# The odd 96 rows of layer 2's gate and up weights: one shared weight, the rest of up in full fp32

## The chip, the cores and the metric

One core of a Trainium2 chip runs the whole program. The metric is device time in microseconds (us) of one execution. The kernel before takes 410.91 us, the median of 3 runs (410.29 to 411.19).

## The reference, cut to what matters

There are 1024 tokens with 512 features, all in fp32. Each of the two layers ends in a layer norm, and each contains a gated feed-forward part. Layer 1's has 1248 hidden rows, layer 2's has 1376, that is 10 full chunks of 128 rows and an odd chunk of 96. Layer 2's weights go through a 4-bit quantisation and back, in blocks of 64 elements.

```python
# layer 1
delta = x @ gate_w.T - local_point
approx_out = approx_up @ local_approx_output.T + sum over m of (delta**m / m! * approx_up) @ fuse_weight[:, :, m-1].T
ffn_out = silu(x @ ffn_gate_w.T) * (x @ ffn_up_w.T) @ ffn_down_w.T        # 1248 rows
x = layernorm(x + approx_out + ffn_out)
# layer 2
dq1, dq2, dq3 = (nf4_quant_dequant(w) for w in (w1, w2, w3))               # 1376 rows
h = silu(x @ dq1.T) * (x @ dq2.T)
x = layernorm(x + h @ dq3.T)
```

## The kernel before

**Products.** Nearly every fp32 product is made of three matmuls in the reduced fp32 format: each operand is split into a high and a low part, and hi·hi, hi·lo and lo·hi are added up in PSUM (`product`, L1291 to L1294). Only one product is done in full fp32 with a single call per piece, `project_up` (L1325 to L1332).

**The order on TensorE.** (1) The pre-stage, (2) layer 1's pairs, (3) layer 1's second stage in two passes, one for each half of the tokens, (4) layer 2's pairs, (5) layer 2's second stage in two passes. A pair is one chunk of hidden rows for one half (512) of the tokens: 4 slices of features times 3 matmuls for gate into one PSUM bank, and the same for up into the next, 24 matmuls in all. Layer 1 has 20 pairs, layer 2 has 22. In layer 2, chunk 10 (96 rows) comes last, as pairs 20 and 21. Its matmuls have 96 columns of weight in place of 128.

**Layer 1's odd chunk** (96 rows, its pairs 0 and 1) is done otherwise. `project_first` (L1316) takes all 96 rows of gate and the last 32 of up as one weight of 128 columns, 12 matmuls for each half. `project_up` then takes up's first 64 rows in full fp32: for each of 4 slices one matmul for either token half, the first half's output on partitions 0 to 63 of a bank, the second's on 64 to 127. It uses the raw weight and the raw x.

**Behind the pairs.** In layer 1, ScalarE applies silu to the gate bank (L680) and VectorE multiplies by up (L917, L920). In layer 2, ScalarE applies silu (L680) and copies up's bank into one of two SBUF buffers `up2` (L597), and GpSimd multiplies (`gate_times_up`, L1254). Pair i of layer 2 may start when the up copy of pair i-2 is done (`bank_free`); the copy of pair i also waits for GpSimd's product of pair i-2. The second stage's first chunk waits before its third tile for the up copy of the last pair.

**The dequantisation** runs beside all this. Each unit of weights (11 units for gate and up, 6 for the third matrix w3) takes 8 steps, called here unit.line, from 0.0 to 16.7. ScalarE draws a line into int8 (`side`, L635 for line 0, L597 for the others), GpSimd clamps it (`level`, L1217; line 0 needs no clamp), VectorE adds it up in PSUM (L881, L885) and after line 7 multiplies by the scale (L888). GpSimd normalises a unit (L1208) three steps ahead of its first. ScalarE may draw at most four steps ahead: step 15.4 waits for VectorE's addition of 15.1. How many steps each engine does ahead of each of its other jobs is written out by hand in the three lists `SHARE`, one entry for each call of `beside()`, which stands first in nearly every job. A finished unit is transposed into PSUM by VectorE (`turn_nf4`, `turn_w3`), and split into high and low parts by ScalarE and VectorE (`split_nf4`, `lo_nf4`, `split_w3`, `lo_w3`).

Of the kernel before, what the change touches and what calls it, by code (L numbers as in the profile page):

```python
# [44 lines left out]
assert 2 * REST - P == LEFT  # L45
# [83 lines left out]
def unit_width(u):  # L129
    if u < C2:  # L130
        return 2 * DC * min(P, F2 - u * P)
    return D * min(2, C2 - 2 * (u - C2))

# [80 lines left out]
def multiplied(i, pool):  # L214
# [15 lines left out]
    "vector": [  # L230
# [5 lines left out]
    "gpsimd": [  # L236
# [24 lines left out]
def build(nc, xT, xN, w_pre, w_fuse, w_in, w_out, consts, w12, w3, w3_end, ident_in, out):  # L261
    with ExitStack() as ctx:  # L262
# [39 lines left out]
        def turned(f):  # L302

            return PS[:, XT_BANK:XT_BANK + 2, :].rearrange("p b n -> p (b n)")[:, 0:unit_width(f)]

# [66 lines left out]
        s_centred, s_root = sem("s_centred"), sem("s_root")  # L372
        s_xtr, s_turn, s_w3turn = sem("s_xtr"), sem("s_turn"), sem("s_w3turn")
# [62 lines left out]
        def h_half(n):  # L436

            i, (kind, c) = SEQ[n]
            a, layer = i % 2, 1 if kind == "out" else 2
            view = h[0:job_rows(SEQ[n][1]), c * TOK + a * HALF:c * TOK + (a + 1) * HALF]  # L440
            return view, (s_h, 2 * c + a + 1) if layer == 1 else product_made(PAIR2[c, a])
# [15 lines left out]
        UP_BANK = 5  # L457

        def parted_up(i):

            _, half, bank = pair_of(1, i)
            return [(slice(LEFT, REST), PS[REST:P, bank, :]),
                    (slice(0, LEFT), PS[half * LEFT:(half + 1) * LEFT, UP_BANK, :])]

        def h_of(layer, i):
            f, half, _ = pair_of(layer, i)
            p = rows1(f) if layer == 1 else rows(f, F2)
            return h[0:p, f * TOK + half * HALF:f * TOK + (half + 1) * HALF]
# [53 lines left out]
        def _(sp):  # L522
# [17 lines left out]
            def load_unit(u):  # L540
                sp.dma_start(unit_read(u), w12[:, u * UW:u * UW + unit_width(u)]).then_inc(s_q[u], 16)
# [53 lines left out]
        def _(act):  # L595
# [76 lines left out]
            def silu(layer, i):  # L672
                beside()
                act.wait_ge(s_pair, i + 1 + (2 * C1 if layer == 2 else 0))
                if layer == 2 and i == 0:

                    act.wait_ge(s_llo_h, 2 * C1)
                dst = h_of(layer, i)
                bank = pair_of(layer, i)[2]
                nc.scalar.activation(dst, PS[0:dst.shape[0], bank, :], ACT.Silu).then_inc(s_silu, 1)  # L680
                if layer == 2 and on_pool(i):
                    k = multiplied(i, True) - 1
                    if k == 0:
# [4 lines left out]
                    copy(up2[0:dst.shape[0], k % 2, :], PS[0:dst.shape[0], bank + 1, :]).then_inc(s_up2, 1)  # L688
# [25 lines left out]
            def split_nf4(f):  # L714
                beside()
                m = rows(f, F2)
                act.wait_ge(s_turn, f + 1)
                wait_nf4_slot(act, f)
                copy(in_slot(w_hi, f, 2 * DC * m), turned(f)).then_inc(s_whi4, 1)
# [110 lines left out]
        def _(dve):  # L830
# [80 lines left out]
            def gate_times_up(layer, i):  # L911
                beside()
                dst = h_of(layer, i)
                dve.wait_ge(s_silu, i + 1 + (2 * C1 if layer == 2 else 0))
                if layer == 1 and i < 2:
                    for to, up_rows in parted_up(i):
# [114 lines left out]
            def lo_nf4(f):  # L1031
                beside()
                m = rows(f, F2)
                n = 2 * DC * m
                dve.wait_ge(s_whi4, f + 1)
                wait_nf4_slot(dve, f)
                v.tensor_tensor(in_slot(w_lo, f, n), turned(f), in_slot(w_hi, f, n).bitcast(F32),
                                ALU.subtract).then_inc(s_wlo4, 1)
# [162 lines left out]
        def _(pool):  # L1201
# [46 lines left out]

            def gate_times_up(i):
# [38 lines left out]
        def _(pe):  # L1288
# [27 lines left out]
            def project_first(half, bank):  # L1316

                wh, wl = (in_slot(w, JOB["in", 0], DC * P).rearrange("p (c m) -> p c m", c=DC) for w in (w_hi, w_lo))
                for c in range(DC):
                    xs = slice(half * HALF, (half + 1) * HALF)  # L1320
                    last = product(PS[:, bank, :], wh[:, c, :], wl[:, c, :], x_hi[:, c, xs], x_lo[:, c, xs], c == 0,
                                   c == DC - 1)
                return last

            def project_up():  # L1325

                w = w_raw(JOB["in", 0])[:, DC * P:2 * DC * REST].rearrange("p (c m) -> p c m", c=DC)
                for c in range(DC):
                    for half in range(2):
                        last = t_.matmul(PS[half * LEFT:(half + 1) * LEFT, UP_BANK, :], w[:, c, :],  # L1330
# [3 lines left out]
            def pair(layer, i):  # L1334
                f, half, bank = pair_of(layer, i)
                m = rows1(f) if layer == 1 else rows(f, F2)
# [21 lines left out]
                if layer == 1 and i < 2:  # L1358
# [188 lines left out]
```

## Time and profile before

| | us |
|---|---|
| three runs | 411.19, 410.91, 410.29 |
| the profiled execution | 410.27 |
| its span | 408.2 |
| TensorE busy in the span | 399.9 (98%) |
| VectorE, ScalarE, GpSimd busy | 324.3, 267.0, 289.8 |

The profiled execution's own time lies 2.07 us above its span, and 0.64 us under the median of the runs. A matmul's duration in a row is its whole way through the array; what one more costs is the distance from one start to the next. Rows of other engines show their own duration, and in brackets the idle time ahead of them and what ended it. In the timeline view an "x2" or "x16" is that many instructions of one form in a row, and the time is that of all.

### The profile page before, as it was taken

How to read it: one execution, taken by the hardware profiler on the slowest of the kernel's cores; microseconds unless marked ns; L12 is line 12 of the kernel's file. 1: busy time of each engine (PE TensorE's matmuls, PEld its weight loads, DVE VectorE, ACT ScalarE, POOL GpSimd, SP SyncE). 2: the span in 40 equal slices, each digit the busy share in tenths (PEclk: the TensorE clock that was granted, in tenths of full speed). 3: DMA queues.
4: the chain of work that ended last, by engine and by line, in shares of the span. 5: the costliest groups of instructions: out<-in, count | busy, mean ns of one | idle time of the engine just before them, and what ended most of it. 6: DMA issues, size and time to landing. Idle time of an engine off the chain costs nothing.

```text
span 408.2 us, 5342 instructions
## 1 busy us (share of the span) xinstructions
PE 399.9 (98%) x1762; PEld 325.8 (80%) x1762; DVE 324.3 (79%) x385; ACT 267.0 (65%) x372; POOL 289.8 (71%) x228
## 2 busy tenths in 40 slices
PE   8999999999999999999999999999999999999993
PEld 6767888888888888888888888888888877888872
DVE  4539889789889996999969799887789989925035
ACT  5574676686685847466955668887769777732613
POOL 0177998986978499737992465799999998954330
PEclk9999999999999999999999999999999999999998
DMA  8993111000104362003052000000000000000202
GB/s 276 406 408 126 53 22 51 28 26 0 53 20 116 92 213 71 26 0 104 1 167 112 0 2 0 0 2 0 2 2 0 2 0 0 2 1 0 104 0 103
DMA packets 10010, 26.42 MB, mean 65 GB/s; under 512 B 1248, under 2 KB 1632, under 8 KB 9728
## 3 DMA queue, kind: packets, MB, share of 16 engines
q1 hardware_dynamic: 9552, 25.30, 17.9%
q10 hardware_dynamic: 432, 0.79, 0.7%
q8 instruction: 14, 0.23, 0.2%
q14 instruction: 12, 0.10, 0.1%
HBM read 23.99 MB, written 2.10 MB: 64 GB/s over the span
## 4 chain that ended last, share of the span: by engine, by line
PE 95%; DVE 1%; POOL 1%; ACT 1%; issue 0%; POOLq 0%; DVEq 0%; ACTq 0%
PE PS L1292 31%; PE PS L1294 31%; PE PS L1293 31%; PE PS L1426 1%; PE PS L1330 1%; PE PS L1420 1%; POOL level L1217 1%; DVE h L917 0%; POOLq L262 0%; PE PS L1435 0%; DVE PS L885 0%; ACT side L635 0%; ACT side L597 0%; PE PS L1438 0%; PE PS L1441 0%
## 5 line engine op out<-in xcount | busy, mean ns | idle before, releaser
L1217 POOL TENSOR_SCALAR level<-side 128x1024 f32<-128x1024 int8 (+2 forms) x119 | 129.0, 1084 | 27.7 <-ACT side L597 15.4
L885 DVE TENSOR_TENSOR PS<-PS,level 128x1024 f32<-128x1024 f32 (+2 forms) x102 | 120.1, 1178 | 22.6 <-POOL level L1217 18.8
L1292 PE MATMUL PS<-x_hi,w_hi 128*128 128x512 f32 (+1 forms) x340 | 132.7, 390 | 0.3 <-DVE h L917 0.3
L1294 PE MATMUL PS<-x_hi,w_lo 128*128 128x512 f32 (+1 forms) x340 | 132.4, 389 | 0.0
L1293 PE MATMUL PS<-x_lo,w_hi 128*128 128x512 f32 (+1 forms) x340 | 132.3, 389 | 0.0
L597 ACT ACTIVATE side<-Q 128x1024 int8<-128x1024 f32 (+2 forms) x84 | 80.6, 998 | 22.1 <-DVE PS L881 18.0
L1247 POOL TENSOR_TENSOR l_lo<-h,l_hi 128x512 fp32r<-128x512 f32 (+1 forms) x42 | 57.3, 1374 | 26.5 <-ACT l_hi L597 25.8
L1292 PEld LDWEIGHTS PS<-x_hi,w_hi 128*128 128x128 f32 (+1 forms) x340 | 63.4, 186 | 15.1 <-issue 0.8
L1294 PEld LDWEIGHTS PS<-x_hi,w_lo 128*128 128x128 f32 (+1 forms) x340 | 63.4, 186 | 13.8
L1293 PEld LDWEIGHTS PS<-x_lo,w_hi 128*128 128x128 f32 (+1 forms) x340 | 63.4, 186 | 13.6
L1293 PE MATMUL PS<-x_lo,l_hi 128*128 128x512 f32 (+1 forms) x144 | 56.1, 389 | 0.0
L1292 PE MATMUL PS<-x_hi,l_hi 128*128 128x512 f32 (+1 forms) x144 | 56.1, 389 | 0.0
L1294 PE MATMUL PS<-x_hi,l_lo 128*128 128x512 f32 (+1 forms) x144 | 56.0, 389 | 0.0
L1236 POOL TENSOR_TENSOR w_lo<-raw,w_hi 128x1024 fp32r<-128x1024 f32 (+2 forms) x15 | 30.8, 2051 | 19.6 <-ACT w_hi L597 19.0
L680 ACT ACTIVATE h<-PS 128x512 f32<-128x512 f32 (+1 forms) x42 | 24.9, 592 | 29.1 <-PE PS L1294 25.9
L1254 POOL TENSOR_TENSOR h<-h,Q 128x512 f32<-128x512 f32 (+1 forms) x22 | 30.3, 1378 | 18.0 <-ACT Q L597 15.7
L597 ACT ACTIVATE l_hi<-h 128x512 fp32r<-128x512 f32 (+1 forms) x42 | 25.9, 626 | 24.9 <-PE PS L1294 24.8
L597 ACT ACTIVATE side<-raw 128x1024 int8<-128x1024 f32 x35 | 35.1, 1058 | 6.1 <-DVE PS L881 6.1
L1292 PEld LDWEIGHTS PS<-x_hi,l_hi 128*128 128x128 f32 (+1 forms) x144 | 27.0, 188 | 6.0 <-issue 0.2
L1292 PE MATMUL PS<-w_hi,l_hi 128*128 128x512 f32 (+1 forms) x80 | 31.5, 394 | 0.2 <-POOL l_lo L1247 0.2
L1294 PEld LDWEIGHTS PS<-x_hi,l_lo 128*128 128x128 f32 (+1 forms) x144 | 27.0, 188 | 5.7
L1293 PEld LDWEIGHTS PS<-x_lo,l_hi 128*128 128x128 f32 (+1 forms) x144 | 27.0, 188 | 5.5
(103 smaller groups left out, 515.2 us busy)
## 6 DMA issues: line engine op xcount, KB each, us to landing
Q<-w SPq DMA_DIRECT2D x10, 512.0 KB, 13.9
raw<-w_in SPq DMA_DIRECT2D x9, 512.0 KB, 9.9
raw<-w_out SPq DMA_DIRECT2D x13, 256.0 KB, 2.7
raw<-w SPq DMA_DIRECT2D x5, 512.0 KB, 3.9
R<-xN SPq DMA_DIRECT2D x2, 1024.0 KB, 6.4
raw<-w_fuse SPq DMA_DIRECT2D x7, 256.0 KB, 2.5
out<-R SPq DMA_DIRECT2D x7, 256.0 KB, 2.0
h<-xT SPq DMA_DIRECT2D x2, 512.0 KB, 7.0
```

Of the source, the lines that this page charges most:

```text
L597: return nc.scalar.activation(dst, src, ACT.Copy, **kw)
L680: nc.scalar.activation(dst, PS[0:dst.shape[0], bank, :], ACT.Silu).then_inc(s_silu, 1)
L885: v.tensor_tensor(total, total, level_of(s), ALU.add).then_inc(s_add, 1)
L1217: g.tensor_scalar(level_of(s), side_of(s), LIMITS[k][1], LIMITS[k][0], ALU.min, ALU.max).then_inc(s_level, 1)
L1236: g.tensor_tensor(lo, w_raw(j)[0:p, 0:n], hi.bitcast(F32), ALU.subtract).then_inc(s_wlo_in if JOBS[j][0] == "in" else s_wlo, 1)
L1247: g.tensor_tensor(lo, view, hi.bitcast(F32), ALU.subtract).then_inc(s_llo_h, 1)
L1254: g.tensor_tensor(dst, dst, up2[0:dst.shape[0], k % 2, :], ALU.mult).then_inc(s_h2, 1)
L1292: t_.matmul(dst, a_hi, b_hi, start=start, stop=False)
L1293: t_.matmul(dst, a_hi, b_lo, start=False, stop=False)
L1294: return t_.matmul(dst, a_lo, b_hi, start=False, stop=stop)
L1330: last = t_.matmul(PS[half * LEFT:(half + 1) * LEFT, UP_BANK, :], w[:, c, :], xT_raw[:, c, half * HALF:(half + 1) * HALF], start=c == 0, s ...
L1420: last = t_.transpose(PS[:, XT_BANK + t % 2, c * P:(c + 1) * P], R[:, t, c * P:(c + 1) * P], ident[:])
```

## The change

Layer 2's odd chunk gets the form that layer 1's has. It becomes unit 4 of layer 2 in the order of work (pairs 8 and 9) in place of the last; its hidden rows keep their place at chunk 10. The numbers of units 5 to 10 now stand for chunks 4 to 9.

- Pair 8 is 12 matmuls for half 0 (gate and 32 rows of up), then 8 fp32 calls for up's other 64 rows, both token halves side by side in bank 3. Pair 9 is 12 matmuls.
- The fp32 calls need x of layer 2 unsplit. GpSimd makes it as x_hi + x_lo in four new jobs (`join_x`, 128x1024 each), placed ahead of its products 0, 1, 3 and 5, and writes it to a part of h that is free then. ScalarE copies the raw 64 rows of up out of PSUM as well (`up2_raw`), and splits only 512 columns in place of 768; so does VectorE.
- The fp32 calls wait for bank 3, that is for the up copy of pair 7, and for the joins.
- ScalarE copies up of pairs 8 and 9 in two pieces each, from two banks.
- The lists `SHARE` are new throughout.

```diff
-SHARE = { ... }
+SHARE = { ... }      # all three lists; the sums stay at 136 steps for each engine
+        x2_raw = h[:, 6 * TOK:(6 + DC) * TOK].rearrange("p (c t) -> p c t", c=DC)
+        up2_raw = h[:, 5 * TOK:5 * TOK + DC * LEFT].rearrange("p (s n) -> p s n", s=2)
...
             def split_nf4(f):
...
+                if f == ODD:
+                    copy(up2_raw, odd_part(turned(f), 2 * P, 2 * (P + LEFT)))
+                    copy(odd_part(dst, 0, 2 * P), odd_part(turned(f), 0, 2 * P)).then_inc(s_whi4, 1)
...
+            def join_x(half, k):
+                beside()
+                pool.wait_ge(s_xl, X_PARTS + TILES * (half + 1))
+                x, hi, lo = (t[:, 2 * k:2 * k + 2, half * HALF:(half + 1) * HALF] for t in (x2_raw, x_hi, x_lo))
+                g.tensor_tensor(x, hi.bitcast(F32), lo.bitcast(F32), ALU.add).then_inc(s_x2raw, 1)
...
             for i in range(2 * C2):
+                if i in (0, 1, 3, 5):
+                    join_x(*{0: (0, 0), 1: (0, 1), 3: (1, 0), 5: (1, 1)}[i])
...
+            def project_up2():
+                w = up2_raw.rearrange("p s (k m) -> p k s m", k=2)
+                for c in range(DC):
+                    pe.wait_ge(s_x2raw, 3 + c // 2)
+                    for half in range(2):
+                        last = t_.matmul(PS[half * LEFT:(half + 1) * LEFT, UP_BANK[2], :], w[:, c // 2, c % 2, :],
+                                         x2_raw[:, c, half * HALF:(half + 1) * HALF], start=c == 0, stop=c == DC - 1)
...
-                if layer == 1 and i < 2:
-                    last = project_first(half, bank)
-                    if half == 0:
+                if is_odd(layer, i):
+                    last = project_odd(layer, slot, half, bank)
+                    if layer == 2 and half == 0:
+                        pe.wait_ge(*bank_free(i - 1))
+                        last = project_up2()
+                    elif half == 0:
                         last = project_up()
```

The first entries of `SHARE["vector"]` (jobs: low part of the first weight, delta, product of pair 0, product of pair 1, kept, product of pair 2) go from 0, 1, 0, 2, 0, 1 to 0, 1, 0, 0, 0, 4. In `SHARE["scalar"]` the entry ahead of layer 1's silu of pair 1 goes from 4 to 2. The entries that stand ahead of the last jobs of layer 2's pairs are these, with the first step that is then still to be done:

| engine, ahead of | before | after |
|---|---|---|
| GpSimd, product 0 of layer 2 | 9.1 | 9.3 |
| GpSimd, product 10 | 12.0 | 11.6 |
| GpSimd, product 19 | 15.4 | 14.6 |
| GpSimd, product 20 | 15.6 | 15.4 |
| ScalarE, silu 19 | 15.4 | 15.0 |
| ScalarE, silu 20 | 15.6 | 15.4 |
| ScalarE, split of w3 chunk 1 | 15.6 | 15.5 |
| ScalarE, silu 21 | 16.1 | 15.6 |
| VectorE, low part of w3 chunk 0 | 15.5 | 15.2 |

## Rows read from the trace of the kernel before

**Rows 1.** The page: busy time; TensorE and its granted clock in 40 slices.
```profile
PE 399.9 (98%) x1762; PEld 325.8 (80%) x1762; DVE 324.3 (79%) x385; ACT 267.0 (65%) x372; POOL 289.8 (71%) x228
...
PE   8999999999999999999999999999999999999993
...
PEclk9999999999999999999999999999999999999998
```
**Rows 2.** The page: the chain that ended last, by line.
```profile
PE PS L1292 31%; PE PS L1294 31%; PE PS L1293 31%; PE PS L1426 1%; PE PS L1330 1%; PE PS L1420 1%; POOL level L1217 1%; DVE h L917 0%; POOLq L262 0%; PE PS L1435 0%; DVE PS L885 0%; ACT side L635 0%; ACT side L597 0%; PE PS L1438 0%; PE PS L1441 0%
```
**Rows 3.** Timeline of TensorE, layer 1's pairs: start, duration, line, operation.
```profile
26.16 0.39 PE L1292 MATMUL PS<-x_hi,w_hi 128*128 128x512 f32 x1
...
31.38 0.39 PE L1294 MATMUL PS<-x_hi,w_lo 128*128 128x512 f32 x1
32.05 0.50 PE L1292 MATMUL PS<-x_hi,w_hi 128*128 128x512 f32 x1 [0.29 <-DVE h L917]
32.39 0.40 PE L1293 MATMUL PS<-x_lo,w_hi 128*128 128x512 f32 x1
```
**Rows 4.** Timeline of TensorE, end of layer 2's pairs.
```profile
329.79 0.39 PE L1292 MATMUL PS<-x_hi,w_hi 128*96 128x512 f32 x1
...
340.87 0.39 PE L1292 MATMUL PS<-w_hi,l_hi 128*128 128x512 f32 x1
...
342.24 0.46 PE L1292 MATMUL PS<-w_hi,l_hi 128*128 128x512 f32 x1
```
**Rows 5.** Timeline of TensorE, layer 1's fp32 part.
```profile
19.41 0.39 PE L1294 MATMUL PS<-x_hi,w_lo 128*128 128x512 f32 x1
19.73 3.65 PE L1330 MATMUL PS<-h,raw 128*64 128x512 f32 x16
23.31 0.50 PE L1292 MATMUL PS<-x_hi,w_hi 128*128 128x512 f32 x1
23.65 0.40 PE L1293 MATMUL PS<-x_lo,w_hi 128*128 128x512 f32 x1
```
**Rows 6.** Line L1330: ns min/median/max, first and last start.
```profile
L1330 PE MATMUL PS<-h,raw x16: 592/592/643, 19.7 to 22.8; 128*64 128x512 f32 x16
```
**Rows 7.** Timeline of ScalarE in layer 1's first pairs.
```profile
24.96 2.94 ACT L597 ACTIVATE side<-Q 128x1024 int8<-128x1024 f32 x3
27.81 0.58 ACT L680 ACTIVATE h<-PS 96x512 f32<-96x512 f32 x1
```
**Rows 8.** Timeline of VectorE in layer 1's first pairs.
```profile
29.33 1.23 DVE L885 TENSOR_TENSOR PS<-PS,level 128x1024 f32<-128x1024 f32 x1 [0.93 <-POOL level L1217]
30.59 1.40 DVE L917 TENSOR_TENSOR h<-PS,h 32x512 f32<-32x512 f32 x2
```
**Rows 9.** Groups by form, whole span: count, busy us and mean ns, idle before.
```profile
L1217 POOL TENSOR_SCALAR level<-side 128x1024 f32<-128x1024 int8 x105 | 118.6, 1129 | 23.3 <-ACT side L597 13.1 <-DVE PS L885 2.4
```
**Rows 10.** Line L1236, GpSimd's subtraction of two SBUF operands: ns min/median/max.
```profile
L1236 POOL TENSOR_TENSOR w_lo<-raw,w_hi x15: 1290/2388/3379, 19.2 to 200.8; 128x1024 fp32r<-128x1024 f32 x9, 128x512 fp32r<-128x512 f32 x5, 96x512 fp32r<-96x512 f32 x1
```
**Rows 11.** Timeline of GpSimd, products 0 and 19 of layer 2's pairs.
```profile
229.80 1.29 POOL L1254 TENSOR_TENSOR h<-h,Q 128x512 f32<-128x512 f32 x1 [12.43 <-ACT Q L597]
...
333.58 1.30 POOL L1254 TENSOR_TENSOR h<-h,Q 128x512 f32<-128x512 f32 x1
```
**Rows 12.** Stretches of layer 2's pairs: span, then busy time of PE, PEld, DVE, ACT, POOL.
```profile
229.00:270.00 41.00, 41.00 (x187) 34.09 (x186) 37.52 (x36) 29.40 (x48) 29.46 (x26) 1.00 0.00 1
270.00:341.00 71.00, 71.00 (x314) 57.36 (x313) 60.20 (x53) 56.20 (x73) 66.93 (x55) 1.00 0.00 1
```
**Rows 13.** Timeline of VectorE near the end of layer 2's pairs.
```profile
329.20 1.23 DVE L888 TENSOR_TENSOR raw<-PS,Q 128x1024 f32<-128x1024 f32 x1
```
**Rows 14.** Timeline of ScalarE, the last two pairs of layer 2.
```profile
337.45 2.01 ACT L597 ACTIVATE side<-raw 128x1024 int8<-128x1024 f32 x2
...
341.07 0.60 ACT L680 ACTIVATE h<-PS 96x512 f32<-96x512 f32 x1 [1.00 <-PE PS L1294]
341.56 0.58 ACT L597 ACTIVATE Q<-PS 96x512 f32<-96x512 f32 x1
```

More of the change, by code:

```diff
@@ L44 @@
 REST, LEFT = F1 % P, 64
-assert 2 * REST - P == LEFT
+assert F2 % P == REST and 2 * REST - P == LEFT
+ODD = 4
+CHUNK_OF = [*range(ODD), C2 - 1, *range(ODD, C2 - 1)]
 KEEP_FROM = 5
@@ L304, in turned, with odd_part @@
             return PS[:, XT_BANK:XT_BANK + 2, :].rearrange("p b n -> p (b n)")[:, 0:unit_width(f)]
+        x2_raw = h[:, 6 * TOK:(6 + DC) * TOK].rearrange("p (c t) -> p c t", c=DC)
+        up2_raw = h[:, 5 * TOK:5 * TOK + DC * LEFT].rearrange("p (s n) -> p s n", s=2)
+        def odd_part(w, first, last):
+            return w.rearrange("p (s n) -> p s n", s=2)[:, :, first:last]
         def term_tile(m, a):
@@ L454, in pair_of, with is_odd, parted_up @@
             return f, half, 2 * ((i + 2) % 3) if layer == 1 else 2 * (i % 2)
-        UP_BANK = 5
-        def parted_up(i):
-            _, half, bank = pair_of(1, i)
+        UP_BANK = {1: 5, 2: 3}
+        def is_odd(layer, i):
+            return pair_of(layer, i)[0] == (0 if layer == 1 else ODD)
+        def parted_up(layer, i):
+            _, half, bank = pair_of(layer, i)
             return [(slice(LEFT, REST), PS[REST:P, bank, :]),
-                    (slice(0, LEFT), PS[half * LEFT:(half + 1) * LEFT, UP_BANK, :])]
+                    (slice(0, LEFT), PS[half * LEFT:(half + 1) * LEFT, UP_BANK[layer], :])]
         def h_of(layer, i):
             f, half, _ = pair_of(layer, i)
+            if layer == 2:
+                f = CHUNK_OF[f]
             p = rows1(f) if layer == 1 else rows(f, F2)
@@ L687, in silu @@
                         act.wait_ge(s_h2, k - 1)
-                    copy(up2[0:dst.shape[0], k % 2, :], PS[0:dst.shape[0], bank + 1, :]).then_inc(s_up2, 1)
+                    if is_odd(layer, i):
+                        for to, up_rows in parted_up(layer, i):
+                            last = copy(up2[to, k % 2, :], up_rows)
+                        last.then_inc(s_up2, 1)
+                    else:
+                        copy(up2[0:dst.shape[0], k % 2, :], PS[0:dst.shape[0], bank + 1, :]).then_inc(s_up2, 1)
             def root_of_variance(layer, g):
@@ L914, in gate_times_up @@
                 dve.wait_ge(s_silu, i + 1 + (2 * C1 if layer == 2 else 0))
-                if layer == 1 and i < 2:
-                    for to, up_rows in parted_up(i):
+                if is_odd(layer, i):
+                    for to, up_rows in parted_up(layer, i):
                         last = v.tensor_tensor(dst[to, :], up_rows, dst[to, :], ALU.mult)
@@ L1314, in project, with project_odd @@
                 return last
-            def project_first(half, bank):
-                wh, wl = (in_slot(w, JOB["in", 0], DC * P).rearrange("p (c m) -> p c m", c=DC) for w in (w_hi, w_lo))
+            def project_odd(layer, slot, half, bank):
+                if layer == 1:
+                    parts = (in_slot(w, slot, DC * P) for w in (w_hi, w_lo))
+                    wh, wl = (w.rearrange("p (c m) -> p c m", c=DC) for w in parts)
+                else:
+                    parts = (in_slot(w, slot, unit_width(ODD)) for w in (w_hi, w_lo))
+                    wh, wl = (odd_part(w, 0, 2 * P).rearrange("p s (k m) -> p k s m", k=2) for w in parts)
                 for c in range(DC):
+                    w_h, w_l = ((w[:, c, :] if layer == 1 else w[:, c // 2, c % 2, :]) for w in (wh, wl))
                     xs = slice(half * HALF, (half + 1) * HALF)
-                    last = product(PS[:, bank, :], wh[:, c, :], wl[:, c, :], x_hi[:, c, xs], x_lo[:, c, xs], c == 0,
-                                   c == DC - 1)
+                    last = product(PS[:, bank, :], w_h, w_l, x_hi[:, c, xs], x_lo[:, c, xs], c == 0, c == DC - 1)
+                return last
+            def project_up2():
[5 more added lines that the diff above has]
+                                         x2_raw[:, c, half * HALF:(half + 1) * HALF], start=c == 0, stop=c == DC - 1)
                 return last
@@ L1329, in project_up @@
                     for half in range(2):
-                        last = t_.matmul(PS[half * LEFT:(half + 1) * LEFT, UP_BANK, :], w[:, c, :],
+                        last = t_.matmul(PS[half * LEFT:(half + 1) * LEFT, UP_BANK[1], :], w[:, c, :],
                                          xT_raw[:, c, half * HALF:(half + 1) * HALF], start=c == 0, stop=c == DC - 1)
@@ L1335, in pair @@
                 f, half, bank = pair_of(layer, i)
-                m = rows1(f) if layer == 1 else rows(f, F2)
+                m = P
                 if layer == 1:
@@ L1509, in by_squares @@
         parts = []
-        for f in range(C2):
+        for f in CHUNK_OF:
             rows_ = [w[f * P:(f + 1) * P].reshape(-1, SQ, 2, DC, BLOCK) for w in ws]
+            if f == C2 - 1:
+                gate, up = rows_
+                parts += [x.transpose(3, 1, 2, 0, 4).reshape(P, -1)
+                          for x in (np.concatenate([gate, up[LEFT // SQ:]]), up[:LEFT // SQ])]
+                continue
             parts.append(np.stack(rows_).transpose(4, 2, 0, 3, 1, 5).reshape(P, -1))
```

26 lines of the change are left out of this document (16 added, 10 removed), and 24 rows, old and new, of the table SHARE.

## The prediction

> **What bounds the kernel now.** I read the page first. TensorE is busy for 399.9 of 408.2 us, in all slices but the first and last, and its granted clock is full, 2.4 GHz, all through [rows 1]. The chain that ended last says the same from the other side: three lines of matmul hold 93% of it [rows 2]. Then I went through TensorE's timeline start by start and looked for distances that are longer than the usual one. In a run of 24 full matmuls, from 26.16 to 31.38 us, the starts lie (31.38-26.16)/23 = 0.227 us apart [rows 3]. Outside the opening, the mode changes and the transposes, only a few places show more: one at 32.05, where TensorE waits for VectorE's product of pair 1 [rows 3], and one of under half a us before the last tiles, which the change doesn't reach. So a matmul taken away is time taken away, if no other engine comes late for it. What is to be asked of the other three is only that: who has how much room ahead of TensorE, above all GpSimd, which fills 66.93 of the last 71 us of layer 2's pairs [rows 12].
>
> **The change part by part.**
>
> Removed: the 48 matmuls with 96 columns, from 329.79 to the start of the next stage at 340.87, 11.08 us [rows 4]. Their spacing, 11.08/48 = 0.231, is no shorter than that of 128 columns: narrower weights bring nothing here.
>
> Added: 24 matmuls of 128 columns, 24 x 0.227 = 5.45 us. Added too: 8 fp32 calls. Layer 1 has the very same form, 8 calls on 64 columns, two token halves on the two halves of a bank. Without it the matmul after 19.41 would have started at 19.64. With it the stream is regular again from 23.65, whose regular forerunner would stand at 23.42 [rows 5]. So it costs 23.42-19.64 = 3.78 us, both changes of form included. The sum on TensorE is 5.45+3.78-11.08 = -1.85 us. Bounds: if operands from other places cost nothing more, 3.58 us for the bare part (19.73 to 23.31), which makes -2.05. If the halves did not run beside each other, twice that; this is a rival below.
>
> What a rule makes of it: the row has 16 records for 8 calls, about 0.22 us apart, although one lasts 592 ns [rows 5, 6]. The Trainium skill, FP8 and Floating Point Precision, TensorE Precision Notes, gives true fp32 four passes. With 8 calls of four passes at the 0.227 us of a full matmul that would be 7.3 us, and the edit would lose. By its page TensorEngine Tiling (Array Packing), Key Properties, different tiles work in parallel and a change of mode drains the engine. The measured 3.78 is half of the four-pass figure plus a little, so the trace agrees with both together.
>
> The first gap in layer 1: pair 3 starts at 32.05 instead of 31.61, and the next start is 0.34 us on instead of 0.227; 32.39-31.38-2x0.227 = 0.56 us are lost [rows 3]. Its cause: VectorE has two steps ahead of the product of pair 1, the second begins at 29.33, after its clamp, and the product comes only at 30.59 [rows 8]. ScalarE's silu of that pair came at 27.81, behind four lines drawn [rows 7]. In the new lists VectorE has none of these steps, and ScalarE two lines fewer, 2.0 us. Pair 1 is through TensorE at about 26.3 (pair 2 starts at 26.16, and the last matmul ends a little later), so silu is done by 26.9 and both product pieces by 28.4, some 3 us before 31.61. I take the whole 0.56; the bounds are 0 and 0.56. What is late next is pair 5, which needs VectorE's product of pair 2, now behind four additions. These end at about 37, when ScalarE's line 4, drawn after silu 2, has passed GpSimd; pair 5 starts at 42.5. That is covered.
>
> GpSimd: four joins of 128x1024 with two operands in SBUF. Such an operation is not in layer 2. The nearest is L1236: median 2.39 us, longest 3.38, and 1.29 for half the width, so twice 1.29 at best [rows 10]. I take 2.4 us, bounds 2.4 and 3.38. The first join lies in the 12.43 us that GpSimd idles ahead of product 0 [rows 11]. The other three are in its stream: 3 x 2.4 plus gaps, 7.4 us. Against this stand clamps: up to product 19 it does 43 steps after product 0's place instead of 51, 7 of these a clamp, at 1.13 us with the gap some 8.3 us [rows 9]. The balance is -0.9 us, while TensorE runs 1.85 us less. Besides, GpSimd is idle for 41.00-29.46 = 11.5 us between 229 and 270 us [rows 12], where the joins fall. So it does not fall behind in total. Transfers are untouched: the same bytes go in at the same places.
>
> Pairs 8 and 9 are short, 12 matmuls and the fp32 part, then 12, so the waits that stand behind them come sooner. Pair 10 starts 12 x 0.227 = 2.7 us after pair 8's end. It needs silu and two copies, 0.5+0.5+0.6 = 1.6 us at ScalarE's pace [rows 14], begun about 0.2 us after that end. There is 0.9 us left, if ScalarE is free then: it has one split and two lines, about 3 us, in the 6.5 us that pair 8 takes. The fp32 part waits 2.7 us after pair 7 for one silu and one copy, 1.1 us. Cost nothing; if ScalarE is in the middle of a line, up to 0.5 us.
>
> The end of layer 2's pairs is the place that I trust least. Call the start of the second stage zero (340.87 before). Its third tile, 1.36 us on, waits for the last up copy: silu started at 0.20, the copy ended at 1.27, and the tile started at 1.37 [rows 4, 14]. So a late silu 21 goes over to TensorE in full. Before, ScalarE was idle for 1.00 us ahead of it. After, it must first draw 15.4, split a chunk and draw 15.5. Step 15.4 waits for VectorE's addition 15.1, which now hangs behind product 19: the product 1.38, clamps 14.6, 14.7 and 15.1 at 1.1 each; behind clamp 14.6, VectorE does two additions, the scaling and addition 15.1, about 1.2 each [rows 8, 13]; then ScalarE 1.0+0.5+1.0 [rows 14]. From product 19's start that is 1.4+1.1+4.7+2.5 = 9.7 us. Pair 19 ends 10.7 us before zero, so product 19 can start at -9.6 at the earliest; before it started at 333.58, at -7.29 [rows 11], with six steps more behind it. From -9.6 silu is ready at +0.1, no stall; from -7.3 it is ready at 2.4, a stall of 2.2 us. GpSimd has three clamps less between products 10 and 19 (21 instead of 24), which makes up 3.4 us against the lag that it had, so I take the early end and a cost of 0.2 us.
>
> The sum: -1.85-0.56+0.2 = -2.2 us. The profiled execution, at 410.27 (span 408.2 and 2.07 around it), would become 408.1. The median of the runs is 0.64 higher, 410.91, and becomes 408.7.
>
> **The rivals.**
>
> (a) The gap at 32.05 stays, or as much is lost at some new place, since the lists are new throughout. An operand that is late by one more clamp ahead of it costs 1.1 us at most [rows 9]. For it: every job of the other engines changes its neighbours. Against: before, it has nearly none of these gaps. Time 408.7+0.6 = 409.3, to 409.9 with a clamp.
>
> (b) The end of the pairs eats the gain: product 19 starts where it did, at -7.3, and the stall is 2.2 instead of 0.2. For it: GpSimd fills 94% of the stretch [rows 12]. Against: the three clamps. Time 408.7+2.0 = 410.7, no change.
>
> (c) Slower: the joins make GpSimd late. Place and price: at 3.38 us each the three joins cost 10.4, 2.1 more than the clamps give back. With TensorE's 1.85 us and nothing taken up by idle time, product 19 starts at -3.3, so silu is 6.2 late and the time is 410.9-2.4+6.2 = 414.7. It decides from a stall of 3.2 us on (product 19 at -6.3), and it needs both long joins and idle time that can't be used; the 11.5 us of idle time speak against it.
>
> (d) The fp32 halves do not run beside each other in layer 2. By the bare part of layer 1 that adds 3.58 us: 408.7+3.6 = 412.3, slower. The layer 1 row is of the same shape and speaks against it. The four-pass rule of the Trainium skill's page named above would bring this time about if taken without the tiles.
>
> (e) The change doesn't do what it says: fewer matmuls, and yet the rows show no shorter stage. Nothing speaks for it; it is in (b).
>
> **How the numbers follow.** Forecast 408.7, within 408.2 to 409.1: 0.50. Rival (a), 409.1 to 410.0: 0.23. (b): 0.13. (c): 0.06. (d): 0.03. The other 0.05: below 408.2, by -2.05 on TensorE and no stall, or a little lost elsewhere. The range of 408.0 to 410.4 holds the first two, part of (b), and the bounds of the terms. A measurement of this kernel can tell 0.2%, 0.82 us, from no change. Faster: forecast, (a) and the rest, 0.76. Same: (b) and a little of (c), 0.14. Slower: 0.10.
>
> **What would show it.** In the profile after: 24 starts 0.227 us apart in pairs 8 and 9 and 16 fp32 records over about 3.6 us between them; no start later than 0.3 us after the one before at pair 3 of layer 1; joins of 2.4 us; the distance of the third tile of the second stage to its second no longer than before; product 19 some 9 us ahead of that stage. It is wrong if TensorE shows a wait at pair 10, at the end of the pairs or at the fp32 part of over 1 us, or if the fp32 part takes 7 us.

## The result, and the profile after

The forecast was 408.7 us, faster. The changed kernel takes 415.57 us (median of 5 runs, 415.36 to 416.86), where the kernel before takes 410.86 (410.25 to 411.19) beside it: a ratio of 1.0129, 95% interval 1.0108 to 1.015. It is slower by 4.7 us. The profiled execution took 415.57, its span is 413.5; before it was 408.2 [rows 1].

The page after, first busy time, then TensorE and its granted clock in 40 slices, then the chain that ended last, by engine:

```profile
PE 401.2 (97%) x1754; PEld 325.0 (79%) x1754; DVE 322.4 (78%) x385; ACT 268.5 (65%) x375; POOL 302.1 (73%) x232
...
PE   8999999999997999999998999999999999999993
...
PEclk9999999999998999999999999999999999999998
...
PE 44%; DVE 20%; POOL 16%; issue 16%; ACT 3%; POOLq 0%; DVEq 0%; ACTq 0%
```

Against [rows 1, 2]: one slice of TensorE has fallen to 7, and in the same slice, the 13th (124 to 134 us), the granted clock has fallen too. The chain that was matmuls for 93% is now matmuls for 44%; VectorE and GpSimd stand in it for 36%. GpSimd's busy time has grown by 12.3 us, of which the four joins, at 2.40 to 2.42 each, are 9.65. The change's own place is as forecast. TensorE's timeline after, pairs 8 and 9 of layer 2 (start, duration, line, operation, and in brackets idle time and what ended it):

```profile
270.61 0.39 PE L1334 MATMUL PS<-x_hi,w_hi 128*128 128x512 f32 x1
...
273.10 0.39 PE L1336 MATMUL PS<-x_hi,w_lo 128*128 128x512 f32 x1
273.50 3.65 PE L1378 MATMUL PS<-h 128*64 128x512 f32 x16
277.08 0.50 PE L1334 MATMUL PS<-x_hi,w_hi 128*128 128x512 f32 x1
277.42 0.39 PE L1335 MATMUL PS<-x_lo,w_hi 128*128 128x512 f32 x1
...
279.94 0.39 PE L1334 MATMUL PS<-x_hi,w_hi 128*128 128x512 f32 x1
```

From 270.61 to 279.94 they take 9.33 us, against 11.08 before [rows 4]. The fp32 part has the same length as that of layer 1 [rows 5]. So 1.75 us are saved here. The loss is in layer 1, which the diff touches only through the lists. The end of its pairs and the start of its second stage, TensorE after:

```profile
124.61 0.40 PE L1334 MATMUL PS<-w_hi,l_hi 96*128 96x512 f32 x1
...
125.77 0.39 PE L1336 MATMUL PS<-w_hi,l_lo 96*128 96x512 f32 x1
128.43 0.50 PE L1334 MATMUL PS<-w_hi,l_hi 96*128 96x512 f32 x1 [2.27 <-DVE h L951]
...
130.16 0.60 PE L1335 MATMUL PS<-w_lo,l_hi 128*128 128x512 f32 x1
130.56 0.63 PE L1336 MATMUL PS<-w_hi,l_lo 128*128 128x512 f32 x1
...
133.55 0.42 PE L1334 MATMUL PS<-w_hi,l_hi 128*128 128x512 f32 x1
```

The third tile waits 2.27 us for VectorE's product of pair 18. Then, from 130.16 to 133.55, eight matmuls start 0.42 us apart instead of 0.227. The stretch from 130.00 to 133.50 (span, then busy time of PE, PEld, DVE, ACT, POOL, then the granted clock, here 0.53) shows it as the lower of TensorE's two levels, 1.2 GHz instead of 2.4, for nearly all of it:

```profile
130.00:133.50 3.50, 3.50 (x10) 2.77 (x9) 3.50 (x4) 2.52 (x4) 3.42 (x3) 0.53 0.59 156
```

Why VectorE is late is in its own timeline. First before, then after:

```profile
120.42 0.68 DVE L920 TENSOR_TENSOR h<-PS,h 128x512 f32<-128x512 f32 x1
121.78 2.57 DVE L885 TENSOR_TENSOR PS<-PS,level 128x1024 f32<-128x1024 f32 x2 [0.68 <-POOL level L1217]
124.38 1.22 DVE L888 TENSOR_TENSOR Q<-PS,amax 128x1024 f32<-128x1024 f32 x1
```
```profile
122.34 0.68 DVE L951 TENSOR_TENSOR h<-PS,h 128x512 f32<-128x512 f32 x1
123.38 1.23 DVE L916 TENSOR_TENSOR PS<-PS,level 128x1024 f32<-128x1024 f32 x1 [0.35 <-POOL level L1250]
124.64 1.22 DVE L919 TENSOR_TENSOR Q<-PS,amax 128x1024 f32<-128x1024 f32 x1
126.00 1.78 DVE L912 SCALAR_TENSOR_TENSOR PS<-side,level 128x1024 f32<-128x1024 int8 x1
127.70 0.68 DVE L951 TENSOR_TENSOR h<-PS,h 128x512 f32<-128x512 f32 x1
```

Before, product 18 is the row at 120.42. After, product 17 is at 122.34 and product 18 at 127.70; TensorE needs it at about 126.0. The scaling that ends unit 5 comes at 124.38 before and at 124.64 after: the steps themselves advance as before. But the new list puts four steps more ahead of product 18 than the old one: the additions 5.6 and 5.7 with that scaling, and 6.0 and 6.1, which are one instruction, the row at 126.00. Three of the four stand between product 17 and product 18. The entries at this place, as the step that is still to be done behind them:

| layer 1, ahead of | before | after |
|---|---|---|
| ScalarE, silu 17 | 5.6 | 6.0 |
| ScalarE, silu 18 | 6.1 | 6.4 |
| VectorE, product 17 | 5.4 | 5.7 |
| VectorE, product 18 | 5.6 | 6.2 |
| GpSimd, low part of the second stage's second chunk | 6.0 | 6.4 |

Part of the wait has a second cause. The addition at 126.00 takes 1.78 us. In before it is the row at 131.81, GpSimd is idle beside it, and it takes 1.22. In after GpSimd is in the middle of four clamps when it starts; they end at 122.30+4.41 = 126.71, and the addition ends 1.07 us later. VectorE before, then GpSimd after:

```profile
131.81 1.22 DVE L881 SCALAR_TENSOR_TENSOR PS<-side,level 128x1024 f32<-128x1024 int8 x1
```
```profile
122.30 4.41 POOL L1250 TENSOR_SCALAR level<-side 128x1024 f32<-128x1024 int8 x4
126.78 2.13 POOL L1269 TENSOR_TENSOR w_lo<-raw,w_hi 128x512 fp32r<-128x512 f32 x1
```

So 0.56 of the 2.27 us are the two engines in each other's way, which the new order brings together here; the last section has more on this.

The whole span falls into stages if the start of each is counted from the start of layer 1's fp32 part (19.73 before, 20.26 after; these 0.5 us lie in the opening, which varied from 19.57 to 20.62 over all the profiles here):

| us from there to | before | after | layer 1's lists as before | best version |
|---|---|---|---|---|
| second stage of layer 1 | 104.96 | 104.35 | 104.97 | 104.35 |
| pairs of layer 2 (the start after the last transposes) | 210.00 | 215.57 | 210.04 | 209.51 |
| second stage of layer 2 | 321.14 | 324.96 | 320.25 | 318.91 |
| last tile's last matmul | 381.47 | 386.24 | 381.54 | 379.48 |

After against before, stage by stage: -0.61, +6.18, -1.75, +0.95, together +4.77. The +6.18 are the wait of 2.43 (2.66 less 0.227), the slow clock at 1.57, a wait of 1.44-0.23 = 1.21 for a low part of GpSimd at 216.93, two small ones of 0.16 and 0.32 at 166.69 and 183.33, 0.34 because the second start behind each of these four waits comes 0.30 to 0.34 us after the first and not 0.227, and 0.15 that is not traced. The +0.95 is at the end of the pairs, TensorE and ScalarE after:

```profile
346.35 0.39 PE L1336 MATMUL PS<-w_hi,l_lo 128*128 128x512 f32 x1
347.54 0.50 PE L1334 MATMUL PS<-w_hi,l_hi 128*128 128x512 f32 x1 [0.79 <-ACT Q L619]
```
```profile
346.41 0.59 ACT L702 ACTIVATE h<-PS 128x512 f32<-128x512 f32 x1
```

Silu 21 starts 1.19 us after the second stage (345.22), and no longer 0.20 [rows 4, 14].

### The profile page after: what moved, and what is told of

It reads as the page before. It is cut to its first block, busy times and chain, and to the rows that moved or that the text cites. A ratio compares the mean times of both kernels' runs of the same rounds, so it can differ in the third digit from the quotient of the medians.

```text
span 413.5 us, 5334 instructions
## 1 busy us (share of the span) xinstructions
PE 401.2 (97%) x1754; PEld 325.0 (79%) x1754; DVE 322.4 (78%) x385; ACT 268.5 (65%) x375; POOL 302.1 (73%) x232
## 4 chain that ended last, share of the span: by engine, by line
PE 44%; DVE 20%; POOL 16%; issue 16%; ACT 3%; POOLq 0%; DVEq 0%; ACTq 0%
PE PS L1334 14%; PE PS L1336 13%; PE PS L1335 13%; DVE PS L916 9%; POOL level L1250 8%; DVE PS L912 4%; POOL h L1294 2%; POOL w_lo L1269 2%; ACT side L619 2%; POOL Q L1241 1%; POOL l_lo L1280 1%; DVE Q L919 1%; PE PS L1487 1%; DVE amax L875 1%; DVE l_lo L985 1%
## 5 line engine op out<-in xcount | busy, mean ns | idle before, releaser
L1250 POOL TENSOR_SCALAR level<-side 128x1024 f32<-128x1024 int8 (+2 forms) x119 | 126.1, 1060 | 26.7 <-DVE PS L916 13.1
L1334 PE MATMUL PS<-x_hi,w_hi 128*128 128x512 f32 x332 | 129.6, 390 | 0.0
L1335 PE MATMUL PS<-x_lo,w_hi 128*128 128x512 f32 x332 | 129.2, 389 | 0.0
L1336 PE MATMUL PS<-x_hi,w_lo 128*128 128x512 f32 x332 | 129.2, 389 | 0.0
L1334 PEld LDWEIGHTS PS<-x_hi,w_hi 128*128 128x128 f32 x332 | 62.3, 188 | 14.5 <-issue 1.6
L1336 PEld LDWEIGHTS PS<-x_hi,w_lo 128*128 128x128 f32 x332 | 62.3, 188 | 13.0
L1335 PEld LDWEIGHTS PS<-x_lo,w_hi 128*128 128x128 f32 x332 | 62.3, 188 | 12.7
L1269 POOL TENSOR_TENSOR w_lo<-raw,w_hi 128x1024 fp32r<-128x1024 f32 (+2 forms) x15 | 35.9, 2392 | 20.0 <-ACT w_hi L619 19.4
L1335 PE MATMUL PS<-w_lo,l_hi 128*128 128x512 f32 (+1 forms) x80 | 31.9, 399 | 0.0
L1336 PE MATMUL PS<-w_hi,l_lo 128*128 128x512 f32 (+1 forms) x80 | 31.9, 399 | 0.0
```

What stands on the lines that cost most here:

```text
L1250: g.tensor_scalar(level_of(s), side_of(s), LIMITS[k][1], LIMITS[k][0], ALU.min, ALU.max).then_inc(s_level, 1)
L1269: g.tensor_tensor(lo, w_raw(j)[0:p, 0:n], hi.bitcast(F32), ALU.subtract).then_inc(s_wlo_in if JOBS[j][0] == "in" else s_wlo, 1)
L1334: t_.matmul(dst, a_hi, b_hi, start=start, stop=False)
L1335: t_.matmul(dst, a_hi, b_lo, start=False, stop=False)
L1336: return t_.matmul(dst, a_lo, b_hi, start=False, stop=stop)
```

## The experiments

All ratios are to the kernel before, run beside each kernel on the same chip, with 95% intervals. "List" means the entries of `SHARE`. The lists of after and of before have the same jobs in the same order, but for the joins.

**1. The odd unit with the lists of before.**

```diff
-SHARE = { lists of after }
+SHARE = { lists of before; 0 ahead of each of the four joins }
```

> The odd unit as changed, with the three lists of the kernel before (the four joins get entries of 0). Theory A, the new lists are what costs: the TensorE saving of 1.7 to 1.9 us comes out, the stall of 2.4 us at layer 1's second stage and the half clock behind it are gone, the gap of 0.56 us at pair 3 is back: 409.0 to 410.0 us. Theory B, the odd unit costs by itself (joins on GpSimd, fp32 reads of h, short pairs): no better than 413.

413.75 us, 1.0083 [1.0068, 1.0098]. The waits of layer 1's second stage and the slow clock are gone, yet it is 3.4 us slower than before, which was not expected: by the number alone this is theory B. Pair 3 of layer 1 waits as before; all the new waits are in layer 2, two of them 1.19 us from start to start (at 274.94 and 325.47). TensorE at the fp32 part and at pair 10:

```profile
268.73 3.65 PE L1381 MATMUL PS<-h 128*64 128x512 f32 x16 [0.39 <-ACT Q L622]
...
276.13 0.47 PE L1337 MATMUL PS<-x_hi,w_hi 128*128 128x512 f32 x1 [0.80 <-issue]
```

They start 0.78 and 1.19 us after the matmul ahead of them. So with the old lists the short pairs are waited for in layer 2, while layer 1 is better off with them. Experiment 3 tests the two together.

**2. The lists of after with the unit of before.**

```diff
-SHARE = { lists of before }
+SHARE = { lists of after, without the joins' entries }
```

> The kernel before with the new lists alone (without the joins' entries), no odd unit. Theory A: the stall at layer 1's second stage is there again with the half clock, and without the odd unit's saving the time is 416 to 417.5 us. Theory B: within 1 us of the kernel before, 410.3 to 412.

420.18 us, 1.0242 [1.0227, 1.0257], some 3 us above what was expected. The wait is at the same place and longer (3.61 us for VectorE's product, then 13 slow matmuls). It is no clean split of the loss: unit 4 is 1024 columns wide here instead of 768, so the steps may take longer than these lists presume; no run tests that. It shows that the new lists alone bring the wait, not how much of it.

**3. After, with the lists of before up to the pairs of layer 2.**

```diff
 SHARE = {
-    layer 1 and its second stage: entries of after
+    layer 1 and its second stage: entries of before
     layer 2: entries of after; ahead of GpSimd's product 0: 5 -> 6, so that the sum stays
```

> The changed kernel with the old lists up to layer 2's pairs, and the new ones from there. Theory A, with the loss in layer 1's part: only the stall of 1 us at the end of layer 2's pairs is left, 409.5 to 410.8 us. If the loss sits in layer 2's part of the lists or in the joins: over 412.

410.57 us, 1.0006 [0.9996, 1.0015]: 5.0 us below after. The stage table shows where: +0.03 in layer 1's second stage in place of +6.18. That layer 1's lists cost the 5 us is shown. Pair 3 of layer 1 waits as before (0.56). What the unit saves, 1.75, is used up by two other waits: the end of layer 2's pairs (0.96), and a new one of 0.97-0.23 = 0.74 just behind the start of layer 2's pairs:

```profile
231.72 0.40 PE L1339 MATMUL PS<-x_hi,w_lo 128*128 128x512 f32 x1
232.69 0.47 PE L1337 MATMUL PS<-x_hi,w_hi 128*128 128x512 f32 x1 [0.57 <-DVE x_lo L1050]
```

GpSimd and ScalarE of this kernel show where that one begins:

```profile
211.88 2.42 POOL L1290 TENSOR_TENSOR h<-x_hi,x_lo 128x1024 f32<-128x1024 f32 x1
214.23 1.93 POOL L1244 TENSOR_TENSOR Q<-Q,rcp 128x1024 f32<-128x1024 f32 x1
```
```profile
216.19 1.15 ACT L660 ACTIVATE side<-Q,line 128x1024 int8<-128x1024 f32 x1 [2.23 <-POOL Q L1244]
...
220.53 0.19 ACT L724 ACTIVATE std<-std 128x2 f32<-128x2 f32 x1
```

The first join stands ahead of GpSimd's normalisation of a weight unit. ScalarE waits 2.23 us for that, draws its lines, and only then takes the square root that x's norm needs, at 220.53 instead of some 219.4. VectorE's x_lo comes a microsecond late.

**4. After, with VectorE's three steps moved behind product 18.**

```diff
-    vector: product 18: 3, product 19: 1
+    vector: product 18: 0, product 19: 4
```

> The changed kernel with one move: VectorE's three steps ahead of layer 1's product of pair 18 go behind it, ahead of product 19. If these three steps are the cause of the stall (2.4 us) and of the half clock behind it (some 1.8 us): 411.3 to 412 us. If VectorE is late there anyhow: over 413.5.

416.48 us, 1.0152 [1.0137, 1.0167], not the 411.3 to 412 expected, and 0.9 us slower than after. The wait goes from the third tile, where product 18 now starts at 124.58, but another comes at the fifth tile, and others stand behind it (1.25 us from start to start at 131.65, 1.48 at 135.52, 1.29 at 166.81). TensorE, then GpSimd:

```profile
129.05 0.47 PE L1337 MATMUL PS<-w_hi,l_hi 128*128 128x512 f32 x1 [1.92 <-issue]
```
```profile
127.69 1.26 POOL L1272 TENSOR_TENSOR w_lo<-raw,w_hi 128x512 fp32r<-128x512 f32 x1
```

The fifth tile is the first of the second chunk, and GpSimd's row is the low part of that chunk's weight. It ends at 128.95, 0.10 us before the tile starts. It stands behind a clamp at 126.57 that waited 1.35 us for VectorE's addition, one of the steps that were moved. In after the same low part ends at 126.78+2.13 = 128.91, so there the wait for product 18 only hid it. So it isn't one entry. On all three engines more steps than before stand at this place ahead of jobs that TensorE needs first (the table of entries above).

**5. Experiment 3, with four of the six steps that GpSimd has between the first join and product 0 moved ahead of the join.**

```diff
-    gpsimd: join (0,0): 0, product 0: 6
+    gpsimd: join (0,0): 4, product 0: 2
```

> As the run with the old lists in layer 1's part, with one move on GpSimd: the first join goes behind the unit-9 normalisation and its clamps instead of ahead of them. Theory A: the join's 2.4 us had held up that normalisation, through it ScalarE's lines and the square root of layer 1's norm, and so TensorE's pair 2 of layer 2 by 0.75 us (0.97 between starts): that gap goes, 409.6 to 409.9 us. Rival: the gap is TensorE's or VectorE's own (slower reads beside a join) and stays: 410.4 to 410.7.

410.55 us, 0.9999 [0.999, 1.0008]: no gain, where 409.6 to 409.9 was expected. ScalarE's lines are now in time, and the wait is still 0.84-0.23 = 0.61 us. The join and the clamp behind it have come to lie beside the small operations of the norm on VectorE, which become slow. VectorE, then GpSimd, of this kernel:

```profile
219.42 0.75 DVE L1016 TENSOR_SCALAR std<-mv 128x2 f32<-128x2 f32 x1
...
220.63 0.64 DVE L1020 TENSOR_TENSOR std<-std 128x2 f32<-128x2 f32 x1
```
```profile
217.74 2.41 POOL L1290 TENSOR_TENSOR h<-x_hi,x_lo 128x1024 f32<-128x1024 f32 x1
220.22 1.04 POOL L1253 TENSOR_SCALAR level<-side 128x1024 f32<-128x1024 int8 x1
```

**6. Experiment 3, with three of the six steps that GpSimd has between products 19 and 20 moved ahead of product 19.**

```diff
-    gpsimd: product 19: 2, product 20: 6
+    gpsimd: product 19: 5, product 20: 3
```

> As the run with the old lists in layer 1's part, with one move on GpSimd: three of the six steps that stand behind product 19 go ahead of it (entries 2, 6 become 5, 3). Theory A, the chain of the prediction (clamp 15.1 behind product 19, VectorE's addition, ScalarE's line 15.4, the last silu): the stall of 0.96 us ahead of the second stage's third tile goes, wholly or to under 0.3: 409.4 to 409.9 us. Rival, GpSimd late in total because of the joins: product 19 comes 3.3 us later and the last products with it, the stall moves to the up copies: no gain, 410.4 or more.

409.91 us, 0.9987 [0.9977, 0.9997]. The clamps that step 15.4 needs now run ahead of product 19, and the wait at the end of the pairs is gone: the third tile of the second stage starts 341.58-340.22 = 1.36 us after the first, as before the change. That is 0.7 us less than experiment 3, or 0.8 if each is taken against the kernel before beside it.

**7. Before, with an early move in layer 1 alone**: the two steps of VectorE ahead of product 1 go behind it, two lines of ScalarE go behind silu 1.

```diff
-    vector: product 1: 2, product 2: 1      scalar: silu 1: 4, silu 3: 1
+    vector: product 1: 0, product 2: 3      scalar: silu 1: 2, silu 3: 3
```

> The kernel before with the layer 1 move alone (VectorE's two steps ahead of the product of pair 1 go behind it, two of ScalarE's lines too). If the 0.56 us at pair 3 is the lists' and worth its full size: 409.8 to 410.0, that is 0.5 to 0.6 under the kernel before. If something later absorbs it: no change.

409.88 us, 0.9981 [0.9973, 0.999]: 0.66 us less. The wait at pair 3 was the order on VectorE and ScalarE (no run separates the two), and this gain can be had without the rest of the change.

**8. Experiment 3 with all three moves (5, 6 and 7).**

> The two moves before together, and in layer 1 VectorE's two steps ahead of the product of pair 1 moved behind it, with two of ScalarE's four lines. If the three gaps are independent: 410.6-0.85-1.0-0.56 = 408.1 us, within 407.9 to 408.6, faster than both kernels. If filling one opens another: 409 to 410.

409.36 us, 0.9964 [0.9952, 0.9977], and not 408.1, since the move of experiment 5 gains next to nothing. Of the three waits only the one at 231.65 is left, 0.58 us.

**9. Experiment 8, with the first join behind the norm.**

```diff
             def join_x(half, k):
                 beside()
                 pool.wait_ge(s_xl, X_PARTS + TILES * (half + 1))
+                if (half, k) == (0, 0):
+                    pool.wait_ge(s_shift, len(NORM_GROUPS))
```

> As the run with the three moves, and the first join also waits for the last shift of layer 1's norm. Theory A: while the join ran, two of VectorE's small operations of that norm took 0.75 and 0.64 us instead of 0.17 and 0.16, which held up pair 2 of layer 2; with the join behind them (GpSimd idles there for 7 us) the gap of 0.81 between starts goes to 0.23: 0.5 to 0.6 us under the run with the three moves, 408.6 to 409.0. Rival: the gap is the chain's own, no change, or the join now meets VectorE's low part of x and makes it late: 409.3 or more.

408.57 us, 0.9939 [0.9926, 0.9953]. This is the best version, faster than both kernels. GpSimd idles 7.43 us until the norm is done, then joins, and x_lo is in time:

```profile
224.99 2.39 POOL L1292 TENSOR_TENSOR h<-x_hi,x_lo 128x1024 f32<-128x1024 f32 x1 [7.43 <-DVE std L1023]
```

In the stage table it is at -0.61, +0.12, -1.74 and +0.24, together -1.99 us.

**10. Experiment 9 with each join done twice**, 9.6 us more for GpSimd.

```diff
+                g.tensor_tensor(x, hi.bitcast(F32), lo.bitcast(F32), ALU.add).then_inc(s_twice, 1)
+                pool.wait_ge(s_twice, twice[0])
                 g.tensor_tensor(x, hi.bitcast(F32), lo.bitcast(F32), ALU.add).then_inc(s_x2raw, 1)
```

> As the run with the join behind the norm, but each of the four joins is done twice, 9.6 us more on GpSimd. If GpSimd has the idle time that the prediction gave it (11.5 us between 229 and 270) the total moves by under 0.5 us. If GpSimd is the second bound behind TensorE, the extra time comes out late as stalls at the products or at the end of layer 2's pairs: 2 us or more.

418.05 us, 1.0174 [1.016, 1.0187]: 9.5 us more than experiment 9. That this is about the 9.6 us of added work is chance, for it is made of two things. From the start of layer 2's pairs to the fp32 part it takes 7.8 us longer, all waits; and the fp32 part itself takes 5.29 instead of 3.59 us from its start to the next matmul, at a granted clock of 0.62, which is 1.7 more. The stretch from the start of the pairs to the fp32 part, of experiment 9, then of this one:

```profile
229.90:267.57 37.67, 37.66 (x168) 30.87 (x166) 34.99 (x31) 27.44 (x45) 31.95 (x23) 1.00 0.00 1
```
```profile
229.90:275.39 45.49, 38.77 (x168) 30.57 (x166) 36.98 (x31) 27.77 (x46) 42.14 (x29) 1.00 0.00 1
```

GpSimd has 10.19 us more work in it (42.14 against 31.95, with some operations lengthened, see the last section), but its idle time only goes from 5.72 to 3.35 us. Of the added work 2.4 us went into idle time, and the rest into the length of the stretch. Between 229 and 270 us GpSimd now waits for nothing, while ScalarE's timeline shows it waiting for GpSimd (3.85 and 4.01 us at single places). TensorE met it at the fp32 part, which waits for the copy of the up product before it:

```profile
275.39 5.35 PE L1387 MATMUL PS<-h 128*64 128x512 f32 x16 [4.90 <-ACT Q L623]
```

**11. Experiment 9 without joins.** The fp32 part reads x's high half alone; x's low part is left out of the 64 rows of up.

```diff
-                    join_x(*{0: (0, 0), 1: (0, 1), 3: (1, 0), 5: (1, 1)}[i])
+                    beside()
...
-                                         x2_raw[:, c, half * HALF:(half + 1) * HALF], ...
+                                         x_hi[:, c, half * HALF:(half + 1) * HALF].bitcast(F32), ...
```

> As the run with the join behind the norm, without any join: the fp32 calls read the high part of x alone in their place, so the low part of x is left out of up's 64 rows. If the joins cost nothing once the lists leave room: within 0.3 us of that run. If contention or GpSimd's load still costs: faster by over 0.5 us.

409.17 us, 0.9954 [0.9941, 0.9966]: 0.6 us more than with joins, which neither theory expected; the intervals overlap. At 231.81 a wait of 0.45 us appears that experiment 9 doesn't have. It comes from what went with the first join, its wait for the norm: a clamp of GpSimd now runs beside the norm, and VectorE's operation on 128x2 takes 1.04 us instead of 0.17. VectorE, then GpSimd:

```profile
219.24 1.04 DVE L1016 TENSOR_SCALAR std<-mv 128x2 f32<-128x2 f32 x1
```
```profile
219.22 1.04 POOL L1253 TENSOR_SCALAR level<-side 128x1024 f32<-128x1024 int8 x1 [1.69 <-DVE PS L919]
```

Apart from that wait, the fp32 part comes 268.06-229.89-0.45 = 37.72 us after the start of the pairs, and with joins 37.67. So four joins, placed as there, cost nothing; four more cost most of their time and the clock besides. The edge lies between, and no run places it nearer.

## Why the prediction was wrong

It was wrong in sign, by 6.9 us. The step that failed is what the new lists cost at the end of layer 1: the sum has it at nothing, and rival (a) prices it at 1.1 us at most; the runs show some 5 to 6 (point 6). By its own steps:

1. *The sum on TensorE, -1.85.* Right: -1.75 measured, stage 3 of the table. The fp32 part costs 3.86 (from 273.33 to 277.19, as worked out in the prediction) and not 3.78, since the fp32 calls start 0.40 after the matmul before them and not 0.32. Rival (d) is out.
2. *The gap at pair 3, -0.56.* Right: from 26.01 to 32.59 after, all starts are 0.227 apart; -0.61 in stage 1, and experiment 7 gives -0.66 by this move alone.
3. *Joins of 2.4 us.* Right in length, 2.40 to 2.42 us. The page after counts them as GpSimd's line L1287. *"The first join lies in the 12.43 us that GpSimd idles ahead of product 0"* was wrong where the lists are before's: it stood ahead of the normalisation, and cost 0.74 us at 231.7 (experiments 3 and 9). After has no wait at that place. That GpSimd, idle for 11.5 us there, *"does not fall behind in total"* holds for four joins (experiment 11), but the idle time is a poor reason. In experiment 10 only 2.4 of 5.7 idle us took up added work. The idle time of experiment 9 between 229 and 270 us is mostly waits for ScalarE's copies and VectorE's scales, 4.6 us; that such waits cannot be filled at will is my reading of it, and no run tests it by itself. Rival (c) had the sign, but not by its cause: the joins are no longer than 2.42 us, and with them in place experiment 9 is faster than before.
4. *Pairs 8 and 9 short, cost nothing.* Right in after: pair 10 shows no wait, the fp32 part starts 0.17 us later than a matmul would. It holds by the new lists only; with the old ones it costs 0.39 and 0.96 us at these two places (experiment 1).
5. *The end of layer 2's pairs, 0.2.* The chain was right and its size was not. Product 19 started 9.23 us ahead of the second stage in after (335.99 against 345.22), and also in experiment 3, whose chain is shown by GpSimd, VectorE and ScalarE:

```profile
330.77 1.29 POOL L1297 TENSOR_TENSOR h<-h,Q 128x512 f32<-128x512 f32 x1
332.15 5.54 POOL L1253 TENSOR_SCALAR level<-side 128x1024 f32<-128x1024 int8 x5
```
```profile
333.23 2.57 DVE L919 TENSOR_TENSOR PS<-PS,level 128x1024 f32<-128x1024 f32 x2 [1.27 <-POOL level L1253]
...
337.19 1.58 DVE L915 SCALAR_TENSOR_TENSOR PS<-side,level 128x1024 f32<-128x1024 int8 x1
```
```profile
338.80 1.06 ACT L622 ACTIVATE side<-raw 128x1024 int8<-128x1024 f32 x1 [1.93 <-DVE PS L915]
```

   VectorE's part was put at 4.7 us (four times about 1.2) and is 338.80-333.23 = 5.57. Of the 0.87 between them, 0.36 is the addition at 337.19, which takes 1.58 where one beside an idle GpSimd takes 1.22 (before, at 131.81): GpSimd's fifth clamp ended at 332.15+5.54 = 337.69, and the addition 1.08 us after that. The remaining 0.51 is gaps between the instructions and 4.7 taken for 4 x 1.22. The other parts of the chain took 0.15 less than forecast, so it is 10.42 us (330.77 to 341.19) instead of 9.7, and product 19 started at -9.23 instead of -9.6. The stall is 0.96 instead of 0.2, and moving the clamps ahead of the product removed it (experiment 6).
6. *Rival (a), as much lost at some new place: "An operand that is late by one more clamp ahead of it costs 1.1 us at most."* This is the step that failed, and it is why the sign was wrong. The mechanism was named and its price was not worked out. The lists are new in all three columns, and I compared them step by step at the start of layer 1 and at the end of layer 2 only. At the end of layer 1 it is not one clamp: VectorE has four steps more than before ahead of product 18, and ScalarE three more ahead of silu 18. So silu 18 comes at 124.34 instead of 119.80 on ScalarE, and product 18 at 127.70 instead of 120.42 on VectorE. It cost 2.43 us, which the slow clock raised by 1.57, and other waits of that stage brought 2.2 more. Putting layer 1's lists back gave all of it back (experiment 3), while mending the one entry gave nothing (experiment 4). My second argument, that before had nearly no such gaps, spoke of lists that were being thrown away.

How much of the 5 us each entry carries stays open. The total by these steps: -1.75-0.61+0.95+6.18 = +4.77, where the forecast had -1.85-0.56+0.2 = -2.2. All but 0.8 of the 7.0 between them is step 6. The best version has the unit, the early move and no costly wait, and its -2.36 us against its own before (408.57 and 410.93; -1.99 between the two profiles) is about the sum that was forecast for the change.

## What to carry to other kernels

When a change replaces a hand-made order, the order is the change: walk the whole list, and at every job that a bottleneck engine waits for compare the number of steps ahead of it, before and after, on every engine; the places where the arithmetic changes are not the places where the order bites. Idle time of an engine that passes work around with two others is less room than it looks: here 2.4 us of 5.7. And where a new operation goes into a full queue, look at what stands right behind it and beside it: one join ahead of a normalisation cost 0.74 us, and behind the norm nothing.

## What the runs showed of the hardware

**TensorE's clock after a wait.** A wait of 2.27 us in after is followed, 1.7 us after work resumed, by 3.4 us at half clock (granted 0.53). In experiment 2 a wait of 3.61 us is followed by 13 slow matmuls, in experiment 10 one of 4.90 by a granted clock of 0.62 from 275.3 to 279.8 us (1.7 us lost). Waits of 1.92 us (experiment 4) and less show none. So a wait on the critical engine may cost more than its length; I had priced none of that. No run shows that the length of the wait alone decides.

**GpSimd and VectorE block each other.** In experiment 5 the 128x2 operation at 219.42 ends at 220.17, with the join (217.74+2.41 = 220.15), and the one at 220.63 ends at 221.27, with the clamp (220.22+1.04 = 221.26); free, as in experiment 9, each takes 0.17 or 0.16 us. In experiment 10 it goes both ways. VectorE, then GpSimd:

```profile
236.34 3.27 DVE L916 SCALAR_TENSOR_TENSOR PS<-side,level 128x1024 f32<-128x1024 int8 x1
```
```profile
236.11 2.40 POOL L1296 TENSOR_TENSOR h<-x_hi,x_lo 128x1024 f32<-128x1024 f32 x1
238.60 1.90 POOL L1254 TENSOR_SCALAR level<-side 128x1024 f32<-128x1024 int8 x1
```

The addition of two SBUF operands starts 0.23 us after the join, ends 1.1 us after the join's end (238.51), and the clamp that started meanwhile lasts 1.90 instead of 1.04. The Trainium skill, SBUF — State Buffer, section "SBUF: two separate sides", has the rule for it: the two engines share a pair of ports under an exclusive lock, held for a whole instruction, taken by VectorE for operations with two SBUF inputs or in a two-port mode. The trace agrees, and adds the size: a join in the wrong place makes a 0.17 us operation one of 0.75, on the path of a norm. It need not be an operation of two inputs on GpSimd's side: the clamp has one, and it did the same to the operation at 219.24 in experiment 11, and to the additions at 126.00 in after and at 337.19 in experiment 3, which end 1.07 and 1.08 us after the clamp. Where VectorE starts first, GpSimd is held: the addition at 112.34 in after takes 1.23 us, and the four clamps from 111.27 on take 5.45 instead of 4.41.
